# An adaLN block with linear attention and a mixture of experts: reordered splits, waits and weight conversion, and zero multiplications in TensorE's idle time

## The reference

```python
h = _layernorm(x) * (1 + ca) + sa
x = x + ga * attention(h)           # 16 heads of 32, relu on q and k
h = _layernorm(x) * (1 + cb) + sb
x = x + gb * ffn(h)                 # 8 experts, top 2, and a shared expert
```

## Time and profile before

| what | us |
|---|---|
| median of 3 runs (lowest, highest) | 1355.58 (1349.45, 1356.57) |
| the profiled execution's own time | 1354.19 |
| its span in the profile | 1352.4 |
| PE busy in the span | 1234.7 (91%) |
| DVE, ACT, POOL busy | 660.1 (49%), 413.1 (31%), 395.2 (29%) |
| mean DMA rate | 162 GB/s |

### The profile page before, as it was taken

The page is one execution under the profiler, slowest core; times in us unless marked ns, Lnnn a source line. Parts: engine busy times, 40 slices in busy tenths (PEclk is TensorE's granted clock), DMA queues, the critical chain, the costliest instruction groups (busy, mean ns, idle before and its releaser), DMA issues.

```text
span 1352.4 us, 25210 instructions
## 1 busy us (share of the span) xinstructions
PE 1234.7 (91%) x9054; PEld 784.3 (58%) x9054; DVE 660.1 (49%) x1382; ACT 413.1 (31%) x869; POOL 395.2 (29%) x367
## 2 busy tenths in 40 slices
PE   6998999999997889878886999999999999989998
PEld 1645565565565656545553555656656665666675
DVE  3646767877876666677764211111111111135455
ACT  2423433433443432422233122222222222212121
POOL 1212555655654433100000111111111111056552
PEclk9999999999999999988897999999999999989999
DMA  5714687897886857633344466565565556399976
GB/s 194 221 47 116 163 195 192 196 224 161 203 216 183 231 157 201 200 101 119 112 131 140 106 141 137 122 140 135 125 137 140 126 135 138 92 245 237 234 215 171
DMA packets 269204, 219.08 MB, mean 162 GB/s; under 512 B 188496, under 2 KB 200784, under 8 KB 268572
## 3 DMA queue, kind: packets, MB, share of 16 engines
q1 hardware_dynamic: 241560, 158.45, 46.4%
q0 software_dynamic: 12848, 35.40, 11.6%
q10 hardware_dynamic: 14680, 23.62, 5.6%
HBM read 116.69 MB, written 56.94 MB: 128 GB/s over the span
## 4 chain that ended last, share of the span: by engine, by line
PE 37%; DMA 9%; DVE 9%; issue 1%; ACT 1%; SPq 0%; ACTq 0%; DVEq 0%; POOLq 0%
PE ps_o L84 6%; PE ps_o L85 6%; PE ps_o L86 6%; PE ps_vs L84 5%; PE ps_vs L86 4%; PE ps_vs L85 4%; DMA xt<-g 4%; DMA out<-xc 2%; DVE tile_is L867 2%; DMA s_ht<-h2t_d 1%; DVE w_all L682 1%; PE ps_y L1393 1%; DVE s_xs L677 1%; PE ps_vh L84 1%; DMA w_stage<-in_w_d 1%
## 5 line engine op out<-in xcount | busy, mean ns | idle before, releaser
L471 POOL DMA_INDIRECT g<-h_d,slot_token x71 | 67.3, 949 | 521.7 <-DMA xt<-g 347.0
L84 PE MATMUL ps_o<-w_all,xt 128*128 x568 | 178.3, 314 | 14.3 <-DMA xt<-g 14.1
L85 PE MATMUL ps_o<-w_all,xt 128*128 x568 | 178.3, 314 | 0.0
L86 PE MATMUL ps_o<-w_all,xt 128*128 x568 | 178.2, 314 | 0.0
L913 DVE TENSOR_TENSOR at<-ps_y,at 128x384 f16<-128x384 f32 x71 | 39.6, 557 | 176.5 <-ACT at L1165 176.5
L908 DVE SCALAR_TENSOR_TENSOR a<-ps_o,a 128x352 f32<-128x352 f32 x71 | 37.2, 525 | 173.7 <-PE ps_o L86 173.7
L1170 ACT ACTIVATE y<-ps_vs,slot_weight 128x512 f32<-128x512 f32 x71 | 48.8, 688 | 230.5 <-PE ps_vs L86 230.5
L84 PE MATMUL ps_qh<-ht,wqkv 128*128 128x128 f16 x512 | 88.6, 221 | 9.6 <-DVE qt L549 7.1
L86 PE MATMUL ps_qh<-ht,wqkv 128*128 128x128 f16 x512 | 88.7, 221 | 0.0
L85 PE MATMUL ps_qh<-ht,wqkv 128*128 128x128 f16 x512 | 88.6, 221 | 0.0
L84 PE MATMUL ps_kh<-s_ht,sh 128*128 128x256 f16 x256 | 72.9, 285 | 13.2 <-DMA s_ht<-h2t_d 11.5
(11 more groups left out here) (240 smaller groups left out, 3179.8 us busy)
## 6 DMA issues: line engine op xcount, KB each, us to landing
y_d<-y SPq DMA_DIRECT2D x71, 256.0 KB, 3.4
w_stage<-in_w_d ACTq DMA_DIRECT2D x64, 176.0 KB, 2.5
xb<-in_x SPq DMA_DIRECT2D x32, 256.0 KB, 3.1
xr<-in_x SPq DMA_DIRECT2D x32, 256.0 KB, 4.0
x_d<-x SPq DMA_DIRECT2D x32, 256.0 KB, 3.0
h_d<-hl SPq DMA_DIRECT2D x32, 256.0 KB, 2.6
h2t_d<-h2t SPq DMA_DIRECT2D x32, 256.0 KB, 3.4
s_ht<-h2t_d SPq DMA_DIRECT2D x32, 256.0 KB, 3.6
```

The source lines that it names most:

```text
L84: nc.tensor.matmul(out, lh, rh, start=first, stop=False, skip_group_check=True)
L85: nc.tensor.matmul(out, lh, rl, start=False, stop=False, skip_group_check=True)
L86: return nc.tensor.matmul(out, ll, rh, start=False, stop=last, skip_group_check=True)
L471: pool.indirect_dma_start(m.g[:, t % 2, :], None, m.h2_d, bass.IndirectOffsetOnAxis(ap=m.slot_token[:, t:t + 1], axis=0)).then_inc(m.gathe ...
```

## The change

Seven edits, in the order of the program:

1. PE multiplies a zero tile (128 x 512, set by POOL) 8 times before it waits for `wmod`, and 14 times between `modulate(1)` and the first keys.
2. The splits of the pieces 0 to 3 move ahead of the first tile's `centre`; of the others, one to two stand before and one to two behind `h_high`/`h_low` of each step. `load_stage(4)` and `(5)` wait for the last `wmod` load; the later loads stand two by two; the second part of `wmod` and the bias loads stand behind `v_high(0)`.
3. In the tail `up(q)` stands before `attend(t)`.
4. In the routing `low(q - 1)` stands before `masks(t)`.
5. The routing's steps are spread over seven q instead of five (bias alone, `name_slots` split off `place`); `masks` run from q = 29, `list_tokens` at q = 46.
6. Some routing tensors move, so that 77 pieces are converted by q = 46 (66 by q = 44 before) and the last 11 in q = 47 to 49 (22 in q = 45 to 50 before).
7. At the end `load_h` moves from SP to ACT, behind `activate(q)` of each chunk's first step, with a buffer wait on `up_done` alone.

```diff
+WARM_UP, KEEP_WARM = 8, 14
+SPLITS_FIRST = {-2: (4,), -1: (6,), 0: (8, 9)}
+SPLITS_LAST = {-2: (5,), -1: (7,), 0: (10, 11)}
-TURNS_FROM = TAIL_STEPS + 5
+TURNS_FROM = TAIL_STEPS + 7
-LAST_PIECES = 3
-SHARED_PIECES = (E - 2) * WP
+LAST_PIECES = 4
+SHARED_PIECES = (E - 1) * WP
...
+    pool.memset(m.k_sb[:, 1, 0, :], 0.0).then_inc(m.idle_ready, 1)
...
@@ vector_program
-        if s == -2:
+        if s == -3:
             for n in range(KC):
                 split_low(n)
...
+        for n in SPLITS_FIRST.get(s, ()):
+            split_low(n)
...
         h2_low(t - 2)
+        for n in SPLITS_LAST.get(s, ()):
+            split_low(n)
...
     for q in range(TAIL_STEPS, EARLY_STEPS):
         multiply(q)
+        low(q - 1)
         for t in list_turn(q):
             masks(t)
-        low(q - 1)
...
@@ scalar_program
+    act.wait_ge(m.wmod_loaded[KC - 1], 16)
     for n in range(KC, STAGE_RING):
         load_stage(n)
+    for n in range(KC):
+        split_high(n)
...
     for q in range(EARLY_STEPS, SH_TILES * CHUNKS):
         activate(q)
+        if q % SH_TILES == 0:
+            load_h(q // SH_TILES + 1)
...
@@ tensor_program
+    def idle(times):
+        for _ in range(times):
+            nc.tensor.matmul(m.ps_v[:, :], m.k_sb[:, 1, 0, 0:P], m.k_sb[:, 1, 0, :], start=True, stop=True)
+
+    pe.wait_ge(m.idle_ready, 1)
+    idle(WARM_UP)
     pe.wait_ge(m.rep_done, KC)
...
     modulate(1)
+    idle(KEEP_WARM)
...
-        attend(t)
         if s >= TILES:
             q = STEPS_PER_SLOT * (s - TILES)
             up(q)
-            if down_due(q):
-                down(q // SH_TILES - 1)
+        attend(t)
+        if s >= TILES and down_due(q):
+            down(q // SH_TILES - 1)
```

More of the change, by code:

```diff
@@ L885, in name_tiles @@
         step(v.tensor_copy(m.eid[:, :], m.eidf[:, :]))
-    beside = {TAIL_STEPS: (pick_first,), TAIL_STEPS + 1: (pick_second,), TAIL_STEPS + 2: (weigh,), TAIL_STEPS + 3: (add_runs,),
-              TAIL_STEPS + 4: (place,), LIST_STEP: (list_tokens,), LIST_STEP - 1: (name_tiles,)}
+    beside = {TAIL_STEPS: (bias_scores,), TAIL_STEPS + 1: (pick_first,), TAIL_STEPS + 2: (pick_second,), TAIL_STEPS + 3: (weigh,),
+              TAIL_STEPS + 4: (add_runs,), TAIL_STEPS + 5: (place,), TAIL_STEPS + 6: (name_slots,), LIST_STEP: (list_tokens,),
+              LIST_STEP - 1: (name_tiles,)}
     sum_logits()
@@ L1088, in scalar_program @@
         if s == -2:
-            for n in range(KC):
-                split_high(n)
-                load_stage(n + STAGE_RING)
-        if s == -1:
-            for n in range(KC, 2 * KC):
-                split_high(n)
-                if n + STAGE_RING < len(m.pieces):
-                    load_stage(n + STAGE_RING)
-        if s == 0:
-            for n in range(2 * KC, 3 * KC):
-                split_high(n)
-            act.dma_start(m.bproj[:, :], m.b_proj.partition_broadcast(B)).then_inc(m.c_loaded, 16)
-            act.dma_start(m.gstage[:, :, :], m.gate_t.rearrange("(k p) e -> p k e", p=P)).then_inc(m.c_loaded, 16)
-            for k in range(KC):
-                act.dma_start(m.wmod[:, k, 2 * C:6 * C], m.wmod_d[k * P:(k + 1) * P, 2 * C:6 * C]).then_inc(m.wmod_loaded[k], 16)
-            act.wait_ge(m.mod_done, 1)
-            act.activation(m.mod[:, 0:C], m.ps_y[0:B, :], ACT.Copy).then_inc(m.mod_copied, 1)
+            load_stage(STAGE_RING)
+            load_stage(STAGE_RING + 1)
+        for n in SPLITS_FIRST.get(s, ()):
+            split_high(n)
         if s == 1:
@@ L1112, in scalar_program @@
             h2_high(t - 2)
-        v_high(s)
+        for n in SPLITS_LAST.get(s, ()):
+            split_high(n)
+        if s == -2:
+            load_stage(STAGE_RING + 2)
+            load_stage(STAGE_RING + 3)
+        if s == -1:
+            load_stage(STAGE_RING + 4)
+            load_stage(STAGE_RING + 5)
+        v_high(s)
+        if s == 0:
+            act.dma_start(m.bproj[:, :], m.b_proj.partition_broadcast(B)).then_inc(m.c_loaded, 16)
+            act.dma_start(m.gstage[:, :, :], m.gate_t.rearrange("(k p) e -> p k e", p=P)).then_inc(m.c_loaded, 16)
+            for k in range(KC):
+                act.dma_start(m.wmod[:, k, 2 * C:6 * C], m.wmod_d[k * P:(k + 1) * P, 2 * C:6 * C]).then_inc(m.wmod_loaded[k], 16)
+            act.wait_ge(m.mod_done, 1)
+            act.activation(m.mod[:, 0:C], m.ps_y[0:B, :], ACT.Copy).then_inc(m.mod_copied, 1)
         o_high(t)
@@ L1178, in scalar_program, with load_h @@
     e_high(SLOT_TILES - 1)
+    def load_h(n):
+        if n < CHUNKS:
+            act.wait_ge(m.up_done, SH_TILES * (n - 1))
+            for u in range(2):
+                act.dma_start(m.s_ht[:, n % 2, u, :, :].rearrange("p j n -> p (j n)"), m.h2t_d[2 * n + u]).then_inc(m.s_ht_loaded[n % 2], 16)
     for q in range(EARLY_STEPS, SH_TILES * CHUNKS):
         activate(q)
+        if q % SH_TILES == 0:
+            load_h(q // SH_TILES + 1)
         if q == EARLY_STEPS:
@@ L1549, in place_buffers @@
     m.run = sb("run", [P, E, TILES], F32)
+    m.best = sb("best", [P, TILES], F32)
+    m.choice = sb("choice", [P, TOP, TILES, E], F32)
+    m.expert_no = sb("expert_no", [P, E], F32)
+    m.expert_far = sb("expert_far", [P, E], F32)
     m.weight = sb("weight", [P, TOP, TILES], F32)
```

31 lines of the change are left out of this document (11 added, 20 removed).

## The result

The changed kernel took 1336.97 us (median of 4 runs, 1331.78 to 1337.95), the kernel before beside it 1352.91: a ratio of 0.9874, 95% interval 0.9833 to 0.9915. A second measurement gave 1335.36 and 0.9829 (0.9798 to 0.9861). So the change is worth 17 or 23 us where 37 were forecast, and the first time lies just above the range, the second just inside it. The profiled execution took 1337.18 us, with a span of 1335.4.

What follows compares the result with a forecast made beforehand. Outside the experts' stage, neither PE nor DVE is full and each waits for the other in turn. Start 7.7, tail 6, routing 15 and end 8 sum to 36.7 us, so 1354.2 becomes 1317.5 us; range 1300 to 1336.

Steps and rivals of the forecast that it cites:

- the tail: Tail: `up` fills the time in which ACT reads the logits; 6 us gained, bounds 3 and 8.
- the attention's way to `project_out`: Tail: `attend` ends one `up` (2.6 us) later in a step, so some transposes are late; 1.7 us lost.
- The start: Start: key splits run while PE multiplies `wmod`, queries start at about 32 us; 7.7 us gained, bounds 5 and 10.
- the second transpose goes out just ahead of them: Start: the 4 MB of `wmod` could spoil the gain, but the second transpose is issued before them; no loss counted.
- The gain is handed on: From 45 to 433 us PE is the bound, so the start's gain of 7.7 us is kept.
- The routing: Routing: shorter waits in chunks 3 to 7 and an earlier start of the experts; 15 us gained, bounds 8 and 19.
- 20 us or more: Routing: sign that the experts' first tile comes this much earlier, with the start's and tail's shift taken off.
- The end: End: `s_ht` loads go out 15 us before they are needed, 10.1 us of waits go; 8 us gained, bounds 3 and 13.
- The rival by which the transfers bind it: End: PE waits for rows of the experts instead of `s_ht`, the end gives nothing; 1325.5 us; chance 12%.
- the change doesn't do what it says: Waits return under other names in tail, routing and end, half of each remains with the start; 1336 us; chance 8%.
- More than forecast: Whole kernel: all upper bounds but one, 10 + 8 + 17 + 12 = 47 us gained; 1307 us; chance 9%.
- The slower rival: Tail: each of eight transposes of `ot` comes 2.5 us late and half clock follows; 1363.5 us; chance 3%.

Runs made afterwards that it cites:

- edit 3 alone: The kernel before with only `up` put before `attend` in the tail; 1359.75 us, ratio 1.0036 to the kernel before.
- the kernel with the early load: The changed kernel with SP issuing the first two loads of `s_ht` ahead of `turn_o` and `turn_h2` at step 31; 1325.34 us, ratio 0.9781.

## Why the prediction was wrong

*The term that failed is the tail*: 6 us forecast; -2.8 and -3.9 in the change's two profiles, where an untouched tail has -0.9 to -2.8; 4.9 us slower (1 to 9) alone. "`up` fills the time in which ACT reads the logits: 8.6 us go" was right. Three steps behind it were not.
- "In the first step `up` waits for `s_ht`, which lands no earlier, and `attend` comes behind it: +0.9 us." I added the wait to what stood before. But `up` in front means that nothing covers the wait for the load any more: `up(0)` starts with its load, 20 to 24 us after the keys of tile 31 in either order, the step's waits rose from 6.8 to 10.5 us, and `attend` came 9 us later. Putting the load in front, and only that, let `up(0)` start at 13.0 us and gave 4.8 us back in the tail's trace.
- "What is late next is the attention's way to `project_out`; I count 1.7 us." It was 4.9, over the 3 us that the prediction itself named as the sign that this term is too large.
- `down(1)` was left out: 4.0 us and 1.7 of half clock. I took PE's list and not ACT's and DVE's, in which `activate(q)` still stood behind `scale2` and everything of DVE behind that. Moving ACT's part took this wait away and made `ot` later; what it is worth in the total is not shown.

*The start* was right in its mechanism: 7.7 forecast, 6.6 alone (4 to 10), queries at 32.75. What failed is the way in which the danger was dismissed, "the second transpose goes out just ahead of them": the second did, at 25.04 us, but the third (tile 2) met the 4 MB, and it took 16.5 us. In four of nine kernels that cost PE over 2.5 us. "The gain is handed on" held within 3 us.

*The routing* was mis-sized: 15 forecast, 14.8 in this profile, but 8.8 (5 to 13) alone by its ratio and 11.8 on the mean of 15 traces. In the traces chunk 3 gave 1.0 to 2.5 (2.4 forecast), chunks 4 to 6 gave 3.3 to 6.8 (6), chunk 7 and the experts' start 1.9 to 6.6, 4.4 on the mean (2 + 4.7). PE's wait for `xt`, 6.8 us where about 4 were foretold, lies in that last part. The sign "20 us or more" for the experts' first tile does not follow from the prediction's own sum for the routing, which is 15.

*The end* was right: 8 forecast, 8.5 alone. The rival by which the transfers bind it is refuted: DMA share 0.87 for 0.84, and no wait for rows came in place of `s_ht`. The rule of the Trainium skill ("DMA: Bandwidth & Descriptors", "Issuing engines are not separate DMA queues") spoke of transfer time; here the position in the list was what changed. The start agrees with it: a transpose issued by SP took 16.5 us beside loads issued by ACT.

*The rival "the change doesn't do what it says"* has the measured time, 1336, but its reason only in the tail; that the number fits is luck. "More than forecast" added 17 and 12 for routing and end, where the prediction's own bounds are 19 and 13. The slower rival did not come: one of the eight transposes of `ot` was 2.5 us late. Its premise, that a rest of 2.5 us brings half clock, does not hold each time either. Behind the late transpose in the change, and behind the same one (2.2 us late) in edit 3 alone:

```profile
465.00:475.00 10.00, 9.59 (x79) 6.59 (x80) 8.06 (x16) 4.91 (x13) 5.45 (x6) 1.00 1.11 287
467.90:471.30 3.40, 3.40 (x10) 1.21 (x9) 2.97 (x3) 1.72 (x5) 2.91 (x3) 0.50 1.02 334
```

Open is how much the experts' stage loses by the edits: it was longer by 0 to 5.7 us in the change and its variants, by 2.4 in a second execution of the kernel before. Open is also how much of the tail's loss in the change is edit 3's, since untouched tails lose up to 2.8.

## What to carry to other kernels

When one engine's list is reordered to fill a wait, look at what stands first in the new order: its operands' loads must be early, and the lists of the engines that read its result must be reordered too. Here the reordering alone cost 5 us (1 to 9), and with both repairs (the early load and ACT's list) the tail was 2.6 to 8.7 us shorter than before in four traces. A gain at one stage moves later work onto transfers that were hidden; look which one comes next for every tile, not for the first. And take a second profiled execution of the kernel before you charge a difference of 5 us to an edit.

## What the runs showed of the hardware

- A transpose of 128 rows, issued 0.02 us ahead of four 1 MB loads by another engine, landed after 16.5 us; the shortest of `ht` in the same stretch took 3.1 us.
- The 16 multiplications by `wmod` took 7.1 to 7.3 us in six of the thirteen kernels with the zero multiplications in front, 8.7 to 9.6 in the others (9.3 in the change), and 9.1 to 10.1 in kernels without them (9.2 in the kernel before). The weight loads show where the time goes: in the change they follow each other every 0.85 us up to 10.4 us and every 0.43 us from there on, in the kernel with the early load every 0.43 us throughout.

```profile
9.50 0.34 PEld L1342 LDWEIGHTS ps_o<-wmod,sct_rep 128*128 128x128 f32 x1 [0.52 <-issue]
10.36 0.20 PEld L1342 LDWEIGHTS ps_o<-wmod,sct_rep 128*128 128x128 f32 x1 [0.52 <-issue]
10.80 0.19 PEld L1342 LDWEIGHTS ps_o<-wmod,sct_rep 128*128 128x128 f32 x1 [0.24 <-issue]
```

  A factor of two is that of the two clock levels, and the step falls together with the first record of the clock in the trace. That record, of full clock, begins at 4.1 to 5.5 us in the six fast kernels, at 9.2 to 10.8 in the seven others, and at 10.0 to 12.0 in those without the zero multiplications. Before its first record the clock column shows 1.00 and says nothing: the zero multiplications of the change start 0.43 us apart under a 1.00, and the first keys, of the same size, 0.22 us apart. What decides between 4 to 5 and 9 to 11 us was not found: the rest between the zero multiplications and the first load was 0.5 us once, with the fast kind, and the others, 0.8 to 1.4 us, went with both kinds.
- Waits of nearly the same length may be followed by half clock or not. The first wait of over 2 us for `ot` in the tail, 2.1 to 2.7 us long, had 3.4 us of half clock behind it in six kernels and none in five, the change among them.
- Two executions of one kernel differed by 5.3 us in PE's account, most of it in the tail (0.9), among the experts (2.4) and at the end (1.8).
